# Two graph-attention layers on one core: whole-pair hops, second buffers for layer 2, and orders dealt anew

## The chip, the core and the metric

The kernel runs on one core of one Trainium2 chip. The metric is the device time of one execution in microseconds (us). TensorE is called PE, VectorE DVE, ScalarE ACT, GpSimd POOL and SyncE SP, as the profile does; PEld is TensorE's loading of weights.

## What is computed

There are 64 graphs of 128 nodes with 256 features, 8 heads of 32, all float32. Layer 0 (the diff's "layer 1") is masked attention with an output projection, a residual and a layer norm; layer 1 ("layer 2") computes probabilities in the same way and then spreads the values four times over the graph:

```python
# layer 0
q, k, v = x @ Wq + bq, x @ Wk + bk, x @ Wv + bv        # per head
attn = softmax(where(adj == 0, -inf, q k^T / sqrt(32)))
x = layernorm(x + (attn v) @ Wo + bo) * gamma + beta
# layer 1, on that x
q, k, v = x @ Wq.T + bq, x @ Wk.T + bk, x @ Wv.T + bv
pros = softmax(where(adj == 0, -16384, q k^T))
z = v
for _ in range(4):                                      # NUM_HOP
    z = 0.9 * pros z + 0.1 * v
out = layernorm(x + z) * gamma + beta
```

## The kernel before

Graphs are taken in 32 pairs, two graphs (b = 0, 1) at a time, so that 256 columns go through a projection. Each engine has a list of its own steps and no scheduler stands behind them: a function `step(t)` (lines 459, 636, 892 and 1031 for PE, ACT, DVE and POOL, and one for SP's loads and stores) names the operations in their order, each for the pair t, t - 1, ... t - 6, and `run` calls it for t = 0 to about 38. Operations whose pair isn't real fall away. So the beginning and the end of the program are the same list with holes in it. Semaphores, one `Count` for each kind of result, carry the order between engines.

For a pair and a layer l the chain is this. `queries`, `keys` and `values` on PE project x (six matmuls a call, since x and W are each split into a rounded high part and a low rest, and three of the four products are made; L326 and L335). `save_q`, `save_k` and `save_v` take the results out of PSUM. `scores` (L375) makes 16 products of 32 rows in the four banks of `psS`; `mask_scores` on DVE (L744, four calls of four heads) adds the mask and finds the maxima; `exp_two` on ACT (L603, eight calls of two heads) makes exponentials and sums; `reciprocals` on DVE (L753) and `probabilities` on POOL (L959) make the probabilities; `turn_probs` on PE (L385) transposes them, four heads a call, and `save_pT` (ACT L612, DVE L760) copies them to `pT`. In layer 0 `attend` (L393) multiplies with v, `save_oh` and `save_ol` split the result, `output` (L335) projects it, `save_y`, `statistics`, `aggregate`, `add_eps` (DVE), `inverse_root` (POOL L972) and `normalise` (DVE L835) make x1, `turn_x1` (L419) transposes it, and `save_x1h`, `save_x1l` split it for layer 1.

In layer 1 a hop is `hop` on PE (L393: for each head, 32 columns of z times pT, 32-wide weights), `save_hop` on ACT (L629, out of PSUM with the factor 0.9), `turn_hop` on PE (L437: two transposes back) and `add_hop` on DVE (L864: adds the restart term `z0s` or, in the fourth, the residual `zf`). All of these are called for one graph of the pair at a time, with 256 of a bank's 512 columns: `hop(j, b, p)`. `restart_term`, `last_term`, `scale_residual`, `shift_residual`, `scale_out`, `shift_out` and `add_bias` are POOL's. The last two pairs are finished by DVE alone (`finish`, L844 and L848).

Four PSUM banks, `F[0]` to `F[3]`, serve everything but scores. A table (lines 159 to 167) deals them out, and before each block PE waits in `free(...)` for the one evacuation that made the bank free. `folds` (L447, L455) multiplies biases into weights once. The seven raw weights lie in one tile `w_raw`, and layer 1's `pT`, `v` and `z0s` have one buffer each: `save_pT(1, ...)` of a pair waits until the last hop of the pair before is done, `save_v(1, p)` until its first hop and restart term are, and `restart_term(p)` for the third hop's sums of pair p - 1.

The order of a round on PE before (pair offsets left out) is: turn_probs(0,0,1); values(0); attend; hop 2; scores(0); turn_hop 2; output; hop 3; four turn_probs(1); values(1,0); hop 0; keys(0,0), values(1,1); turn_x1; keys(0,1); queries(0); turn_hop 3 and 0, one graph each; queries(1); keys(1,0); turn_hop 3 and 0 of the other graph; keys(1,1); turn_probs(0,1,1); hop 1; scores(1); turn_hop 1; turn_probs(0,1,0) and (0,0,0).

Of the kernel before, what the change touches and what calls it, by code (L numbers as in the profile page):

```python
# [13 lines left out]
HD = D // H  # L14
# [65 lines left out]
def two_layers(nc, x, x_t, adj, w, rows, cols, ident_d, out):  # L80
    ctx = ExitStack()
    with ctx:
# [15 lines left out]
        def over_jb(name):  # L98
            return [[count(f"{name}{j}_{b}") for b in range(2)] for j in range(NUM_HOP)]
# [5 lines left out]
        w_raw = sb("w_raw", [128, NW, C, D])  # L105
# [19 lines left out]

        xh = [sb(f"xh{l}", [128, C, T], F32R) for l in range(2)]
# [3 lines left out]
        v = [sb(f"v{l}", [128, 2, D]) for l in range(2)]  # L130
# [6 lines left out]
        pT = [sb(f"pT{l}", [128, 2, H, N]) for l in range(2)]  # L137
# [12 lines left out]
        z0s = sb("z0s", [128, 2, D])  # L150
        zf = [sb(f"zf{i}", [128, 2, D]) for i in range(4)]
        hT = [sb(f"hT{i}", [128, 2, C, N]) for i in range(2)]
# [6 lines left out]
        ps_q = [F[3], F[2]]  # L159
        ps_k = [F[1], F[0]]  # L160
        ps_v = [F[1], F[0]]
        ps_T = [[[F[0], F[2]], [F[3], F[2]]],
                [[F[0], F[3]], [F[2], F[1]]]]
        ps_av, ps_wo, ps_x1 = F[3], F[2], F[2]
        ps_h = [[F[3], F[2]], [F[1], F[3]], [F[2], F[0]], [F[1], F[3]]]
        ps_u = [[F[1], F[0]], [F[1], F[2]], [F[0], F[1]], [F[1], F[3]]]
        ps_fold_bo, ps_fold = F[3], F[1]
# [6 lines left out]
        avr = [count(f"av{b}_ready") for b in range(2)]  # L174
        wor = count("wo_ready", 2)
        x1r = count("x1T_ready")
        hr = over_jb("hopT_ready")
        zr = over_jb("hop_ready")
# [5 lines left out]
        hT_s = over_jb("hopT_saved")  # L184
# [16 lines left out]
        z_s = over_jb("hop_saved")  # L201
# [34 lines left out]

        def run(step, begin, end):
            for t in range(begin, end):
                step(Pair(t))
# [8 lines left out]
        def _(sp):  # L248
# [18 lines left out]
            def load_w(i):  # L267
                sp.dma_start(w_raw[:, i, :, :], w[i].rearrange("(c p) o -> p c o", p=128)).then_inc(w_in[i], 16)
# [12 lines left out]
            load_w(0)  # L281
            load_w(1)
            sp.dma_start(col[:, :, :], cols).then_inc(col_in, 16)
            load_adj(P0)
            load_w(2)
# [10 lines left out]
            def step(t):  # L296
                load_xt(t + 2)
                store(t - 5)
                load_x(t + 1)
                load_adj(t + 2)  # L300

            run(step, 0, PAIRS + 5)
# [4 lines left out]
        def _(pe):  # L307
# [9 lines left out]
            def weight(p, i):  # L317
                if p.is_(0):
                    pe.wait_ge(wh_s, i + 1)
                    pe.wait_ge(wl_s, i + 1)  # L320
# [68 lines left out]
            def spread(l, b, dst, o, src, done):  # L389
                for c in range(C):  # L390
                    for g in range(G):
                        h = G * c + g
                        last = nc.tensor.matmul(dst[32 * g:32 * g + 32, o + c * N:o + (c + 1) * N],  # L393
                                                src[:, b, h * HD:(h + 1) * HD], pT[l][:, b, h, :],
                                                start=True, stop=True)
                last.then_inc(done.sem, 1)

            def attend(b, p):
                if p.real:
                    pe.wait_ge(v_s[0].sem, v_s[0].at(p))  # L400
                    pe.wait_ge(pT_s[0][b][0].sem, pT_s[0][b][0].at(p))
                    pe.wait_ge(pT_s[0][b][1].sem, pT_s[0][b][1].at(p))
                    spread(0, b, ps_av, b * D, v[0], avr[b])
# [19 lines left out]
            def hop(j, b, p):  # L423
                if p.real:
                    if j:
                        pe.wait_ge(z_s[j - 1][b].sem, z_s[j - 1][b].at(p))
                    else:
                        pe.wait_ge(v_s[1].sem, v_s[1].at(p))
                        pe.wait_ge(pT_s[1][b][0].sem, pT_s[1][b][0].at(p))
                        pe.wait_ge(pT_s[1][b][1].sem, pT_s[1][b][1].at(p))  # L430
                    spread(1, b, ps_h[j][b], 0, z[p.parity] if j else v[1], hr[j][b])

            def turn_hop(j, b, p):
                if p.real:
                    pe.wait_ge(hT_s[j][b].sem, hT_s[j][b].at(p))
                    for c in range(C):
                        last = nc.tensor.transpose(ps_u[j][b][:, c * 128:(c + 1) * 128], hT[p.parity][:, b, c, :],  # L437
                                                   ident[:, :])
                    last.then_inc(zr[j][b].sem, 1)

            def folds():

                pe.wait_ge(sc_s, 1)
                for n, i in ((0, 3), (1, 6)):
                    pe.wait_ge(w_in[i], 16)
                    for kc in range(C):
                        last = nc.tensor.matmul((ps_fold_bo, ps_fold)[n][:, :D], spread_col[:, n, kc, :],  # L447
                                                w_raw[:, i, kc, :], start=(kc == 0), stop=(kc == C - 1))
                    last.then_inc(fold_r, 1)
                for n, i in ((0, 4), (1, 5)):  # L450
                    pe.wait_ge(w_in[i], 16)
                    for c in range(C):
                        o = D + n * C + c
                        for kc in range(C):
                            last = nc.tensor.matmul(ps_fold[:, o:o + 1], w_raw[:, i, kc, c * 128:(c + 1) * 128],  # L455
                                                    col[:, BE0c, kc:kc + 1], start=(kc == 0), stop=(kc == C - 1))
                last.then_inc(fold_r, 1)

            def step(t):
                free((z_s[1][1], t - 5), (pT_s[0][1][1], t - 2))  # L460
                turn_probs(0, 0, 1, t - 2)
                free((z_s[1][0], t - 5), (hT_s[1][0], t - 5), (z_s[0][0], t - 5), (z_s[3][0], t - 6), (k_s[0], t - 1))
                values(0, 0, t - 1)
                values(0, 1, t - 1)
                free((pT_s[0][1][0], t - 2))
                attend(0, t - 2)
                attend(1, t - 2)
                free((pT_s[0][0][0], t - 2), (k_s[1], t - 3), (z_s[0][1], t - 5))
                hop(2, 1, t - 5)
                free((pT_s[0][0][1], t - 2), (z_s[1][1], t - 5))  # L470
# [606 lines left out]
```

## Time and profile before

| what | value |
|---|---|
| three runs | 815.98, 816.67 and 817.33 us, median 816.67 |
| the profiled execution | 817.31 us, its span 815.4 us |
| mean granted TensorE clock over the span | 0.983 of full |
| busy: PE, ACT, DVE, POOL | 94%, 84%, 81%, 68% of the span |
| chain that ended last | PE 91%, DVE 4%, issue 3%, ACT 1%, DMA 1% |
| DMA | 34.19 MB, mean 42 GB/s |

The span is the time from the first to the last instruction of the program in the profile. Matmuls are pipelined, so that two may overlap in the rows: their starts are to be compared, not their ends. Idle time is counted in front of the instruction that ended it, with the engine and line that it waited for.

### The profile page before, as it was taken

To read this page: it belongs to the slowest core of one execution; us is meant where nothing else is said; L and a number is where in the kernel's file an instruction comes from. 1 tells how busy PE (TensorE), PEld (TensorE's weight loads), DVE (VectorE), ACT (ScalarE), POOL (GpSimd) and SP (SyncE) were. 2 spreads that over 40 slices of the span, in tenths; PEclk is the share of its full clock that TensorE was granted. 3 is DMA by queue.
4 is the path that set the end of the run, shared out by engine and by line. 5 is a ranking of instruction groups with operands and counts; after the bars stand their busy time and mean duration, and the time that the engine had idled before them with its cause. 6 is when DMAs were issued, how large, how long until landed. Compare 5 with 4: busy or idle time off the path is not lost.

```text
span 815.4 us, 33295 instructions
## 1 busy us (share of the span) xinstructions
PE 769.7 (94%) x11544; PEld 710.5 (87%) x11544; DVE 658.4 (81%) x3253; ACT 687.0 (84%) x2698; POOL 554.7 (68%) x417
## 2 busy tenths in 40 slices
PE   5678999999999999999999999999999999998873
PEld 5677999999999999999999999999999999997762
DVE  2578778888888888888888888888888888888745
ACT  3558999889998998899899989898998898989661
POOL 0245666777877777777777777787777777777662
PEclk9789999999999999999999999999999999999998
DMA  6101100111011111110111111011111110110001
GB/s 217 34 27 41 28 23 2 48 48 46 11 41 48 47 48 47 49 36 15 47 49 47 49 48 47 17 33 48 47 48 48 47 48 16 35 35 28 16 22 46
DMA packets 33252, 34.19 MB, mean 42 GB/s; under 512 B 2368, under 2 KB 28864, under 8 KB 33088
## 3 DMA queue, kind: packets, MB, share of 16 engines
q1 hardware_dynamic: 33088, 32.06, 12.9%
q8 instruction: 96, 1.57, 0.9%
q14 instruction: 68, 0.56, 0.2%
HBM read 23.67 MB, written 8.39 MB: 39 GB/s over the span
## 4 chain that ended last, share of the span: by engine, by line
PE 91%; DVE 4%; issue 3%; ACT 1%; DMA 1%; SPq 0%; POOLq 0%; DVEq 0%; ACTq 0%
PE psF L326 23%; PE psF L393 19%; PE psF L335 17%; PE psF L385 14%; PE psS L375 8%; PE psF L437 8%; PE psF L419 2%; DMA w_raw<-in_w 1%; DVE z L864 0%; ACT ex L603 0%; DVE sm L744 0%; ACT hT L629 0%; DVE w_lo L689 0%; ACT oh L621 0%; DVE y L791 0%
## 5 line engine op out<-in xcount | busy, mean ns | idle before, releaser
L603 ACT ACTIVATE ex<-sm,nmax 128x128 f32<-128x128 f32 x1024 | 396.9, 395 | 13.4 <-DVE nmax L744 13.4
L959 POOL TENSOR_TENSOR pr<-ex,rec 128x1024 f32<-128x1024 f32 x128 | 244.5, 1911 | 109.2 <-DVE rec L753 105.5
L744 DVE CUSTOM_DVE_ANT_0 sm<-psS,mask 128x128 f32<-128x128 f32 x1024 | 226.1, 284 | 4.6 <-PE psS L375 4.6
L603 ACT ACTIVATION_READ_ACCUMULATOR ex<-sm,nmax 128x1 f32 x1024 | 198.1, 193 | 0.0
L612 ACT ACTIVATE pT<-psF 128x512 f32<-128x512 f32 x192 | 104.7, 598 | 47.4 <-PE psF L385 47.4
L385 PE MATMUL psF<-ident,pr 128*128 128x128 f32 x1024 | 132.2, 278 | 5.0 <-issue 3.8
L326 PE MATMUL psF<-xh,w_hi 128*128 128x256 f32 x512 | 114.9, 306 | 15.5 <-DVE w_lo L685 7.6
L385 PEld LDWEIGHTS psF<-ident,pr 128*128 128x128 f32 x1024 | 115.4, 143 | 12.2 <-issue 11.4
L629 ACT ACTIVATE hT<-psF 128x256 f32<-128x256 f32 x256 | 95.1, 387 | 22.1 <-PE psF L393 16.7
L972 POOL TENSOR_TENSOR rstd<-ve,mhalf 128x2 f32<-128x2 f32 x64 | 55.5, 867 | 83.9 <-DVE ve L823 83.9
L864 DVE TENSOR_TENSOR z<-psF,z0s 128x256 f32<-128x256 f32 x192 | 76.5, 412 | 41.2 <-PE psF L437 41.0
L393 PE MATMUL psF<-pT,z 128*32 128x128 f32 x3072 | 103.4, 275 | 3.8 <-DVE z L864 3.2
L326 PE MATMUL psF<-xh,w_lo 128*128 128x256 f32 x512 | 104.3, 286 | 0.0
L326 PE MATMUL psF<-xl,w_hi 128*128 128x256 f32 x512 | 104.3, 286 | 0.0
L326 PEld LDWEIGHTS psF<-xh,w_hi 128*128 128x128 f32 x512 | 79.9, 194 | 21.8 <-issue 20.2
L393 PEld LDWEIGHTS psF<-pT,z 128*32 128x32 f32 x3072 | 80.6, 110 | 14.6 <-issue 9.3
L437 PE MATMUL psF<-ident,hT 128*128 128x128 f32 x512 | 82.0, 280 | 7.1 <-ACT hT L629 2.1
L744 DVE DVE_READ_ACCUMULATOR2_ANT nmax<- 128x1 f32 x1024 | 85.1, 83 | 0.0
L326 PEld LDWEIGHTS psF<-xl,w_hi 128*128 128x128 f32 x512 | 80.8, 194 | 0.0
L326 PEld LDWEIGHTS psF<-xh,w_lo 128*128 128x128 f32 x512 | 80.5, 194 | 0.0
L375 PE MATMUL psS<-kT,qT 32*128 32x128 f32 x2048 | 75.1, 283 | 0.9 <-DVE kT L733 0.9
L375 PEld LDWEIGHTS psS<-kT,qT 32*128 32x128 f32 x2048 | 63.0, 186 | 13.6 <-issue 13.5
(68 smaller groups left out, 1422.2 us busy)
## 6 DMA issues: line engine op xcount, KB each, us to landing
xt_in<-in_x_t SPq DMA_DIRECT2D x32, 256.0 KB, 3.3
x_in<-in_x SPq DMA_DIRECT2D x32, 256.0 KB, 3.7
out<-o_t SPq DMA_DIRECT2D x30, 256.0 KB, 3.0
adj_in<-in_adj SPq DMA_DIRECT2D x32, 128.0 KB, 3.0
w_raw<-in_w SPq DMA_DIRECT2D x7, 256.0 KB, 4.8
row<-in_rows SPq DMA_DIRECT2D x1, 768.0 KB, 6.4
out<-o_t SPq DMA_DIRECT2D x4, 128.0 KB, 1.7
ident<-in_ident SPq DMA_DIRECT2D x1, 64.0 KB, 3.8
```

What stands on the lines that cost most here:

```text
L326: last = nc.tensor.matmul(dst[:, c * T:(c + 1) * T], w_p[e][:, i, kc, c * 128:(c + 1) * 128], x_p[a][:, kc, :], start=(n == 0 and kc == 0) ...
L335: last = nc.tensor.matmul(dst[:, b * D:(b + 1) * D], x_p[a](kc), w_p[e][:, i, kc, :], start=(n == 0 and kc == 0), stop=(n == 2 and kc == C ...
L375: last = nc.tensor.matmul(psS[:, o:o + N], qT[l][r, c, b * N:(b + 1) * N], kT[l][r, c, b * N:(b + 1) * N], start=True, stop=True)
L385: last = nc.tensor.transpose(ps_T[l][b][c][:, g * N:(g + 1) * N], pr[l][:, b, G * c + g, :], ident[:, :])
L393: last = nc.tensor.matmul(dst[32 * g:32 * g + 32, o + c * N:o + (c + 1) * N], src[:, b, h * HD:(h + 1) * HD], pT[l][:, b, h, :], start=Tru ...
L437: last = nc.tensor.transpose(ps_u[j][b][:, c * 128:(c + 1) * 128], hT[p.parity][:, b, c, :], ident[:, :])
L603: e = nc.scalar.activation(ex[l][:, b, h, :], sm[l][:, b, h, :], ACT.Exp, scale=-1.0, bias=nmax[l][:, b, h:h + 1], accum_out=tot[l][:, b, ...
L612: nc.scalar.activation(pT[l][:, b, G * c:G * c + G, :], ps_T[l][b][c][:, :].rearrange("p (g n) -> p g n", g=G), ACT.Copy).then_inc(pT_s[l] ...
L629: nc.scalar.activation(hT[p.parity][:, b, :, :], ps_h[j][b][:, :D].rearrange("p (c n) -> p c n", c=C), ACT.Copy, scale=1.0 - ALPHA).then_i ...
L744: last = nc.vector.tensor_tensor_reduce(sm[l][:, b, h, :], psS[:, o:o + N], mask[p.parity][:, b, :], -1.0, BIG, ALU.add, ALU.min, nmax[l][ ...
L864: nc.vector.tensor_tensor(dst[:, b, :], ps_u[j][b][:, :D], add[:, b, :], ALU.add).then_inc(z_s[j][b].sem, 1)
L959: nc.gpsimd.tensor_tensor(pr[l][:, b, :, :], ex[l][:, b, :, :], rec[l][:, b, :].unsqueeze(2).broadcast_to([128, H, N]), ALU.mult).then_inc ...
```

## The change

- `w_raw` shrinks to weights 4 to 6. Weights 0 to 3 are loaded into what is later the second buffer of `pT` (`raw(i)`). Layer 1 gets two each of `pT`, `v` and `z0s`; the second `v` and `z0s` are `w_raw[1]` and `w_raw[0]`, once the weights have been read. The waits of `save_pT(1)`, `save_v(1)` and `restart_term` now look back two pairs.
- `hop`, `turn_hop`, `save_hop` and `add_hop` take both graphs of the pair in one call with a whole bank: 32 matmul records, four transposes, one operation on 512 columns. `attend` does so too. Semaphores per graph go.
- `save_hop(0)`, and layer 0's `save_k`, go from ACT to DVE; all eight `save_pT` and `save_x1h` go to ACT. `make_mask` is told which maxima read the mask last.
- Banks are dealt anew. Each compute engine's list is now a written-out `begin()`, a `step(t)` for t = 7 to 31 and a written-out `end()`; hops lie up to seven pairs back and stores nine. SP keeps its step with `store(t - 9)`.
- In the rounds, hop 1 of one pair and hop 3 of the pair before stand on either side of `attend`, and hop 0 and hop 2 of two pairs are neighbours.

```diff
-        w_raw = sb("w_raw", [128, NW, C, D])
+        w_raw = [sb(f"w_raw{i}", [128, C, D]) for i in range(4, NW)]
...
+        def raw(i):
+            if i < 4:
+                return pT1[1][:, i // 2, 4 * (i % 2):4 * (i % 2) + 4, :].rearrange("p (c o) n -> p c (o n)", c=C)
+            return w_raw[i - 4][:, :, :]
...
+        v1 = [sb("v1", [128, 2, D]), w_raw[1]]
+        z0s = [sb("z0s", [128, 2, D]), w_raw[0]]
+        pT1 = [sb(f"pT1_{i}", [128, 2, H, N]) for i in range(2)]
...
+        ps_q = [F[0], F[3]]
+        ps_k = [F[2], F[1]]
+        ps_v = [F[0], F[2]]
+        ps_T = [[[F[3], F[3]], [F[2], F[1]]],
+                [[F[0], F[3]], [F[1], F[3]]]]
+        ps_av, ps_wo, ps_x1 = F[1], F[1], F[1]
+        ps_h = [F[0], F[3], F[2], F[2]]
+        ps_u = [F[2], F[0], F[0], F[3]]
...
+            def hop(j, p):
+                if p.real:
+                    if j:
+                        pe.wait_ge(z_s[j - 1].sem, z_s[j - 1].at(p))
+                    else:
+                        pe.wait_ge(v_s[1].sem, v_s[1].at(p))
+                        for saved in pT_s[1][0] + pT_s[1][1]:
+                            pe.wait_ge(saved.sem, saved.at(p))
+                    spread(pT1[p.parity], ps_h[j], z[p.parity] if j else v1[p.parity], hr[j])
...
+            def step(t):
+                free((z_s[2], t - 7))
+                values(0, 0, t - 2)
+                free((mx[0][1][0], t - 3))
+                scores(1, t - 4)
+                free((pT_s[0][0][1], t - 3))
+                turn_probs(0, 0, 0, t - 3)
...
+                turn_probs(0, 1, 1, t - 3)
+                values(0, 1, t - 2)
+                free((pT_s[0][0][0], t - 3))
+                hop(1, t - 6)
+                free((pT_s[0][1][1], t - 3))
+                attend(t - 3)
+                free((pT_s[0][1][0], t - 3))
+                hop(3, t - 7)
+                free((mx[1][1][0], t - 4))
+                scores(0, t - 2)
+                free((hT_s[1], t - 6))
+                turn_probs(1, 0, 1, t - 5)
+                free((v_s[0], t - 2))
+                turn_hop(1, t - 6)
+                free((ol_s, t - 3))
+                output(0, t - 3)
+                output(1, t - 3)
+                free((z_s[1], t - 6))
+                queries(0, 0, t - 1)
...
+                values(1, 1, t - 4)
+                free((y_s, t - 3))
+                turn_probs(1, 1, 0, t - 5)
...
+                free((v_s[1], t - 4))
+                keys(0, 0, t - 1)
+                keys(0, 1, t - 1)
+                free((pT_s[1][1][1], t - 5))
+                turn_hop(3, t - 7)
+                free((pT_s[1][1][0], t - 5))
+                turn_x1(t - 3)
+                free((pT_s[1][0][0], t - 5))
+                hop(0, t - 5)
+                free((k_s[0], t - 1))
+                hop(2, t - 6)
+                free((z_s[3], t - 7))
+                queries(1, 0, t - 3)
+                queries(1, 1, t - 3)
+                free((x1l_s, t - 3))
+                keys(1, 0, t - 3)
+                free((hT_s[0], t - 5))
+                turn_hop(2, t - 6)
+                keys(1, 1, t - 3)
+                free((hT_s[2], t - 6))
+                turn_hop(0, t - 5)
+                free((q_s[1], t - 3))
                 turn_probs(0, 0, 1, t - 2)
...
+            def end():
...
+                hop(3, Pair(31))
+                free((z_s[3], Pair(30)))
+                turn_hop(3, Pair(31))
+
+            begin()
+            run(step, 7, PAIRS)
+            end()
...
             def step(t):
...
+                save_q(0, t)
                 add_eps(0, t - 2)
+                normalise(1, 0, t - 8)
+                mask_scores(0, 1, 1, t - 1)
                 normalise(0, 1, t - 2)
                 normalise(0, 0, t - 2)
+                reciprocals(1, 0, t - 3)
+                normalise(1, 1, t - 8)
+                save_k(0, t)
+                aggregate(1, t - 7)
+                add_hop(3, t - 6)
                 save_x1l(t - 2)
+                save_hop(0, t - 4)
                 reciprocals(0, 0, t - 1)
+                add_eps(1, t - 7)
```

PE's `begin()` starts with queries, keys and values of pair 0 and its scores, then the folds; DVE's starts with make_mask, save_q, save_k and maxima of pair 0 ahead of `save_fold`. In DVE's `end()`, `finish` of pair 30 stands ahead of `add_hop(3, Pair(31))`.

## Rows read from the trace of the kernel before

**Rows 1.** The page, part 1: busy time, share of the span, instructions.

```profile
PE 769.7 (94%) x11544; PEld 710.5 (87%) x11544; DVE 658.4 (81%) x3253; ACT 687.0 (84%) x2698; POOL 554.7 (68%) x417
```

**Rows 2.** Busy time by stage: stage, its length, engines, TensorE's granted clock, DMA share, GB/s.

```profile
core 0: us, PE busy (x) PEld busy (x) DVE busy (x) ACT busy (x) POOL busy (x), PEclk, DMA share, GB/s
7.60:47.10 39.50, 27.40 (x226) 25.47 (x226) 19.76 (x80) 18.00 (x63) 6.56 (x4) 0.83 0.28 93
...
111.10:742.40 631.30, 631.30 (x9717) 587.63 (x9716) 542.42 (x2722) 572.45 (x2266) 468.76 (x349) 1.00 0.13 40
742.40:778.00 35.60, 28.75 (x463) 25.05 (x464) 27.26 (x130) 25.86 (x109) 24.72 (x20) 1.00 0.03 10
```

**Rows 3.** Timeline of TensorE (start us, us taken): the transposes of x1.

```profile
47.15 1.09 PE L419 MATMUL psF<-ident,xn 128*128 128x128 f32 x4
...
67.86 0.60 PE L419 MATMUL psF<-ident,xn 128*128 128x128 f32 x4
...
88.13 0.60 PE L419 MATMUL psF<-ident,xn 128*128 128x128 f32 x4
...
111.13 0.60 PE L419 MATMUL psF<-ident,xn 128*128 128x128 f32 x4
...
719.70 0.60 PE L419 MATMUL psF<-ident,xn 128*128 128x128 f32 x4
```

**Rows 4.** Timeline of TensorE, one round: equal neighbours are merged.

```profile
448.22 1.47 PE L385 MATMUL psF<-ident,pr 128*128 128x128 f32 x12
...
450.49 0.40 PE L335 MATMUL psF<-w_lo,xh 128*128 128x256 f32 x2
450.73 0.40 PE L335 MATMUL psF<-w_hi,xl 128*128 128x256 f32 x2
451.06 1.08 PE L393 MATMUL psF<-pT,v 128*32 128x128 f32 x32
451.96 1.06 PE L393 MATMUL psF<-pT,z 128*32 128x128 f32 x32
452.94 1.17 PE L375 MATMUL psS<-kT,qT 32*128 32x128 f32 x32
...
456.06 1.08 PE L393 MATMUL psF<-pT,z 128*32 128x128 f32 x32
457.07 1.97 PE L385 MATMUL psF<-ident,pr 128*128 128x128 f32 x16
...
462.23 0.60 PE L419 MATMUL psF<-ident,xn 128*128 128x128 f32 x4
462.58 0.48 PE L326 MATMUL psF<-xh,w_hi 128*128 128x256 f32 x2
```

**Rows 5.** Timelines of ScalarE and VectorE in the same round: what reads PSUM.

```profile
448.85 1.58 ACT L612 ACTIVATE pT<-psF 128x512 f32<-128x512 f32 x3 [0.95 <-PE psF L385]
...
448.87 0.28 DVE L744 CUSTOM_DVE_ANT_0 sm<-psS,mask 128x128 f32<-128x128 f32 x1
...
452.24 0.20 DVE L753 RECIPROCAL rec<-tot 128x8 f32<-128x8 f32 x1
...
462.87 0.69 DVE L768 CAST xh<-psF 128x512 fp32r<-128x512 f32 x1 [0.47 <-PE psF L419]
```

**Rows 6.** Timelines of GpSimd and VectorE: probabilities, and a weight split beside one.

```profile
28.90 1.89 POOL L959 TENSOR_TENSOR pr<-ex,rec 128x1024 f32<-128x1024 f32 x1 [1.84 <-DVE rec L753]
...
29.14 2.20 DVE L685 TENSOR_TENSOR w_lo<-w_raw,w_hi 128x512 fp32r<-128x512 f32 x1 [0.32 <-ACT w_hi L557]
...
452.52 1.96 POOL L959 TENSOR_TENSOR pr<-ex,rec 128x1024 f32<-128x1024 f32 x1 [1.27 <-DVE rec L753]
```

**Rows 7.** Timelines of several engines: the beginning and the end.

```profile
4.84 0.69 DVE L685 TENSOR_TENSOR w_lo<-w_raw,w_hi 128x512 fp32r<-128x512 f32 x1 [0.18 <-ACT w_hi L557]
...
28.10 0.39 ACT L603 ACTIVATE ex<-sm,nmax 128x128 f32<-128x128 f32 x1
...
806.30 0.63 PE L437 MATMUL psF<-ident,hT 128*128 128x128 f32 x4 [0.91 <-ACT hT L629]
...
807.42 0.47 DVE L844 SCALAR_TENSOR_TENSOR o_t<-y,mv,row 128x256 f32<-128x256 f32 x1
```

More of the change, by code:

```diff
@@ L96, in over_bc, with over_j @@
             return [[[count(f"{name}{l}_{b}{c}") for c in range(C)] for b in range(2)] for l in range(2)]
-        def over_jb(name):
-            return [[count(f"{name}{j}_{b}") for b in range(2)] for j in range(NUM_HOP)]
+        def over_j(name):
+            return [count(f"{name}{j}") for j in range(NUM_HOP)]
         P0, P1 = Pair(0), Pair(1)
@@ L148, in two_layers @@
         xn = [sb(f"xn{i}", [128, 2, D]) for i in range(2)]
-        z0s = sb("z0s", [128, 2, D])
         zf = [sb(f"zf{i}", [128, 2, D]) for i in range(4)]
-        hT = [sb(f"hT{i}", [128, 2, C, N]) for i in range(2)]
+        hT = [sb(f"hT{i}", [128, 2 * C, N]) for i in range(2)]
         z = [sb(f"z{i}", [128, 2, D]) for i in range(2)]
@@ L235, in two_layers, with turn @@
         block = ctx.enter_context(nc.Block())
+        W_ORDER = (0, 1, 2, 3, 4, 5, 6)
+        def turn(i):
+            return W_ORDER.index(i) + 1
         def run(step, begin, end):
@@ L297, in step @@
                 load_xt(t + 2)
-                store(t - 5)
+                store(t - 9)
                 load_x(t + 1)
                 load_adj(t + 2)
-            run(step, 0, PAIRS + 5)
+            run(step, 0, PAIRS + 9)
             for p in (Q, R):
@@ L679, in _ @@
+            begin()
+            run(step, 7, PAIRS)
+            end()
         @block.vector
@@ L689, in split_w @@
                         last = nc.vector.scalar_tensor_tensor(
-                            out=w_lo[:, i, kc, :], in0=w_raw[:, i, kc, :], scalar=col[:, GA0c, kc:kc + 1],
+                            out=w_lo[:, i, kc, :], in0=raw(i)[:, kc, :], scalar=col[:, GA0c, kc:kc + 1],
                             in1=w_hi[:, i, kc, :].bitcast(FP32), op0=ALU.mult, op1=ALU.subtract)
@@ L796, in statistics @@
                     if l:
[L797 to L798 removed]
+                        dve.wait_ge(z_s[NUM_HOP - 1].sem, z_s[NUM_HOP - 1].at(p))
                     else:
@@ new lines, in step @@
+            def step(t):
+                mask_scores(0, 1, 0, t - 2)
+                save_q(1, t - 3)
+                add_hop(2, t - 6)
+                reciprocals(0, 1, t - 2)
+                save_k(1, t - 3)
+                add_hop(0, t - 5)
+                statistics(1, t - 7)
+                mask_scores(1, 0, 0, t - 3)
+                reciprocals(1, 1, t - 4)
+                mask_scores(1, 1, 1, t - 3)
+                mask_scores(1, 0, 1, t - 3)
+                mask_scores(1, 1, 0, t - 3)
+                make_mask(t - 1)
+                split_lo(t)
+                save_ol(t - 2)
+                mask_scores(0, 0, 1, t - 1)
+                add_hop(1, t - 5)
+                mask_scores(0, 0, 0, t - 1)
+                save_y(t - 2)
+                statistics(0, t - 2)
@@ L949, in _ @@
+            begin()
+            run(step, 7, PAIRS)
+            end()
         @block.gpsimd
@@ L1049 @@
+            begin()
+            run(step, 7, PAIRS)
+            end()
 def kernel(**inputs):
```

1473 lines of the change are left out of this document (1171 added, 302 removed).

## The prediction

> **What bounds the kernel now.** I read the page's busy times first, then the stages, then TensorE's timeline. TensorE (PE) is busy 94% of the span, ScalarE (ACT) 84%, VectorE (DVE) 81% [rows 1]. By stage it is plainer: from 111 to 742 us PE is busy all of the time at full clock, while ACT is busy 572 and DVE 542 of 631 us; before 47 us and after 742 us it is not, and its clock is below full before 47 us [rows 2]. The transposes of x1, one block a pair, stand at 111.13 and 719.70 with 26 pairs between: 23.41 us a round, PE's own sum [rows 3]. The kernel is three parts: a filling to about 111 us, rounds of 23.41, a draining after 742. Thirty-two rounds and the folds (3.4 us) are 752.5 us of PE work; the other 63 of the 815.4 us are standing, slow clock and the ends.
>
> A round has 14 projections of six matmuls (P), 52 transposes, five blocks of 32-wide matmuls over both batches (attention and four hops, H) and two score blocks (S). From start to start: two matmuls of P take 0.24 us, so P 0.71; twelve transposes last 1.47 and four 0.60, so 0.109 each, four 0.44 (T). An H block that stands alone takes 1.01 (456.06 to 457.07), two in a row 1.88 (451.06 to 452.94): so H is 0.87 and **each run of H blocks costs 0.14 beside it**. S takes 1.10 (its 1.17 less the 0.07 by which an H's 1.08 is over its spacing). Going from P into such a block costs 0.09 (450.73 to 451.06 is 0.33 in place of 0.24); sixteen transposes behind an H last 1.97 where twelve last 1.47, 0.50 for four in place of 0.44, so the return to T costs 0.06 [rows 4]. Summed with four runs this gives 23.3, the round but for rounding.
>
> **Part 1, the round's order on PE.** No matmul is added or dropped. Before, the tiled blocks stand in four places: (A, hop 2, S), (hop 3), (hop 0), (hop 1, S). After, in three: (S), (hop 1, A, hop 3, S), (hop 0, hop 2). Two H runs fewer, 0.28; one entry from P fewer, 0.09; one return to T fewer, 0.06. That is 0.42 a round: 22.99. The 25 rounds of the new step give 10.5; counting the places in the written-out beginning and end in the same way, PE's whole work falls by 12.6. S alone behind P has no row in the stretch of rounds; its price lies between nothing saved (a further 0.1 lost) and 0.1 gained, 2.5 us in all either way, and I take the S of rows 4.
>
> **Part 2, whether the others keep up.** ACT loses eight hop evictions of 256 and layer 0's two of keys and gets three of 512, two of pT and x1's high part: a 512 eviction steps 0.49 (three in 1.58) [rows 5], so 2.9 us go in; a 256 one steps between half of that and all of it, so 2.5 to 4.9 go out. I take the middle, about 0.7 less. DVE gets save_k(0) and save_hop(0), gives up two pT and x1h, and sums 512 four times in place of 256 eight times: at least one 0.6 less. GpSimd (POOL) does the same. So per round neither is asked for more than before, which was 572 and 542 of 631 us, 21.2 and 20.1 of 23.41 [rows 2], and both fit in 22.99. SP's queue has the same DMAs; stores come up to four rounds later and each output tile is still taken only after its store.
>
> What matters is each hand-over. A PSUM reader starts 0.29 us after the block's end (462.58 to 462.87), sixteen masked maxima take 3.37 (448.87 to 452.24), a DVE 512 takes 0.60 to 0.69 [rows 4, 5]. With the prices above I laid the new round on a ruler (values(0,0) at 0): S1 0.9 to 2.0, hop 1 4.1, A 5.0, hop 3 5.9, S0 6.95 to 8.0, turn of hop 1 8.45, queries 10.3, values(1,1) ends 13.1, transposes 13.1 to 14.5, keys 14.5, turn of hop 3 15.9, x1 16.3 to 16.8, hop 0 16.9, hop 2 17.7, layer 1's queries 18.84, turn of hop 0 22.1. The tight ones: **S0** needs layer 1's maxima, 2.1 + 3.4 + a reciprocal 0.1 = 5.7 of 6.95; **queries** need hop 1's sum, 8.9 + 0.3 + 0.7 = 9.9, and their weights load from 10.1: 0.2 spare; **keys** need v1 saved, 13.1 + 0.3 + 0.6 = 14.0 of 14.3; **layer 1's queries** need x1's low part: ACT 17.04 to 17.55, DVE (behind keys 16.8, aggregate 17.0, hop 3's sum 17.6) 17.6 to 18.3, with loading from 18.6: 0.3 spare. Attention behind four pT evictions has 0.8, hop 2's bank 0.6. So no wait is left on PE, but four margins are 0.2 to 0.3. The second buffers of pT, v and z0s are costed at nothing: no row of a round shows PE waiting, and what they bring is the right to hold hops of pair p while pair p + 1 is saved; without them the order could not be.
>
> **Part 3, the filling.** The queries come first and need only weight 0, whose low part is ready at 5.5 (4.84 + 0.69) [rows 7]; PE started at 7.6 [rows 2]: 2 gained. Then DVE does all of pair 0's maxima before the folds, so exps end at about 21 in place of 28.5 (28.10 + 0.39) [rows 7]. Walking on with the same prices: probabilities by POOL to 23.8, raw weights rounded to 24.0, four pT to 26.5, attention 26.6, output from 29.3, y behind the weight splits 32.3, statistics and root 34.3, x1 of pair 0 at **35.3** in place of 47.15. Pair 1 at 53.1 in place of 67.86 and pair 2 at 72.2 in place of 88.13 [rows 3]: between them PE stands at score blocks for maxima and at x1 for the root, 0.5 to 1.2 a time. From there 26.2 us of PE work reach the first round; with 1 for clock and small waits it begins at 99.5.
>
> **Part 4, the draining.** The written-out end holds 84.3 us of PE work to its last turn. Waits, by the same prices: scores of pair 31 for maxima 0.5, x1 of pair 30 for its root 1.0, keys of pair 31 for x1 0.7, and the last hops 5.6: a whole-pair hop is H, 0.3 + 0.5 on ACT, T, 0.3 + 0.7 on DVE, 3.2 us, where pair 30's hop beside it fills 1.3, and at the very end nothing does. So 92.1. Then sum, statistics, root, two finishing operations a batch and the store. From the last turn to the end it was 9.1 (806.30 to 815.4) [rows 7]; pair 30's finishing, four DVE operations of about 0.47 that stood in this path for 1.8, now comes ahead of the last sum: 7.6, and 0.3 for that sum's delay. Total 100.0.
>
> **Sum.** 99.5 + 25 x 22.99 + 100.0 = 774.3. Waits that a hand walk misses can only add; I add 2.2: a span of 776.5. The profiled run took 817.31 for its span of 815.4, 1.9 more: 778.4, and the median of the runs lies 0.6 below it: **778 us** against 816.7. Of the 39 gained, 12.6 are PE's own prices and 26 the two ends.
>
> **The rivals.** (a) *The margins fail a little*: a hand-over of 0.2 spare comes late by 0.2 to 0.6 each round, 5 to 15 us: 783 to 793. For it: four such places, and DVE and ACT both serve each x1. Against: 2 to 4 us of slack in both engines' sums. (b) *The ends give half*: the filling's clock stays low longer (0.83 there now [rows 2]) or a fixed order stands for one late engine; 13 us back: 791.
>
> (c) *The lock, on the slower side.* DVE operations with SBUF operands alone and POOL's work exclude each other here: w_lo that takes 0.69 took 2.20 when it began inside a probabilities operation of 28.90 to 30.79 [rows 6, 7]. In the new round the second output normalise(1,1) stands right behind reciprocals(1,0), which releases POOL's 1.9 us probabilities(1,0), and ahead of keys, hop 3's sum and x1's low part. If POOL wins that race, DVE is 1.9 late there, the 0.3 spare is used up and layer 1's queries wait 1.6: 25 x 1.6 = 40 us, 818. It decides from 1.55 a round on (38.7 / 25). Against it: DVE issues at once, while POOL starts 0.08 behind the reciprocal's end (452.24 + 0.20 to 452.52) [rows 5, 6], so DVE should get in first.
>
> The Trainium skill, SBUF — State Buffer, section "SBUF: two separate sides", says that the port pair of these two engines is an exclusive lock and that whichever starts first has it for its whole instruction. By that rule the trace agrees (2.20 for 0.69), and rival (c) would give about 818 wherever POOL is first.
>
> **How the numbers follow.** Forecast (span within 6 us of the sum) 0.62, its own range 771 to 786; (a) 0.17; (b) 0.13; (c) 0.04; better than 770, 0.04. The range 770 to 795 takes in the forecast, (a) and most of (b) and leaves out (c). About 0.2% is what a measurement can tell here, and only (c) comes near it or past: faster 0.95, within 0.01, slower 0.04.
>
> **What would show it.** x1's blocks at 35, 53 and 72 us and then 22.99 apart; PE busy 100% from about 100 to 690 at clock 1.0; last turn some 7.6 ahead of the end. Part 1 is wrong if an unwaited round isn't 22.99; part 2 if PE's gaps recur each round; (c) if w-type DVE operations of 2 us recur each round.

## The result and the profile after

The changed kernel took **783.1 us** (median of four runs, 782.6 to 786.1) against 816.8 of the kernel before: a ratio of 0.960, 95% interval 0.9585 to 0.9612. The forecast was 778.0 with a range of 770 to 795. The profiled run was the longest of the four, 786.14 us with a span of 784.0, and a second profile of the same kernel has a span of 781.1. Of the 2.9 us between the two, 2.3 arise in the first 38 us, so both are shown.

The page, part 1, of the kernel after:

```profile
span 784.0 us, 32528 instructions
...
PE 754.1 (96%) x11544; PEld 710.6 (91%) x11544; DVE 637.1 (81%) x3093; ACT 665.7 (85%) x2570; POOL 547.8 (70%) x417
```

Against [rows 1], PE has the same 11544 matmuls and is busy 15.6 us less in a span that is 31.4 us shorter; ACT's and DVE's busy times are 21 us less each. Next, busy time by stage, first of the profiled run, with the columns of [rows 2]: filling to pair 0's x1, filling to the first generic round, 25 rounds, two stretches of the draining.

```profile
5.60:37.90 32.30, 29.20 (x250) 26.88 (x250) 23.80 (x102) 21.49 (x82) 7.44 (x5) 0.89 0.43 140
37.90:103.10 65.20, 61.99 (x804) 57.08 (x805) 51.23 (x261) 55.49 (x223) 38.88 (x28) 1.00 0.12 34
103.10:677.20 574.10, 574.10 (x9001) 547.00 (x8999) 482.41 (x2393) 514.45 (x2003) 424.83 (x319) 1.00 0.14 40
677.20:736.00 58.80, 57.45 (x951) 53.17 (x950) 49.20 (x246) 52.52 (x200) 45.53 (x37) 1.00 0.08 25
736.00:775.00 39.00, 30.79 (x541) 26.19 (x542) 23.40 (x81) 19.83 (x65) 30.17 (x25) 0.96 0.09 29
```

And the same stages of the second profile:

```profile
5.60:35.70 30.10, 25.80 (x251) 23.44 (x252) 23.60 (x103) 21.16 (x82) 7.43 (x5) 1.00 0.46 145
35.70:100.70 65.00, 62.05 (x804) 57.11 (x805) 50.27 (x260) 55.57 (x223) 38.94 (x28) 1.00 0.12 35
100.70:674.70 574.00, 574.00 (x8999) 546.90 (x8998) 482.32 (x2392) 514.42 (x2002) 425.36 (x319) 1.00 0.14 40
```

In the rounds PE is busy for 574 of 574 us at full clock: a round is 22.96 us. ACT works 20.6 and DVE 19.3 us in each, so both stay below it. Between the two profiles the first stage differs most: at clock 0.89 it took 2.2 us longer than at 1.00, for the same 250 matmuls.

The timeline of PE, the transposes of x1 (start us, us taken), of the kernel after:

```profile
37.93 0.63 PE L436 MATMUL psF<-ident,xn 128*128 128x128 f32 x4
56.46 0.69 PE L436 MATMUL psF<-ident,xn 128*128 128x128 f32 x4 [0.15 <-issue]
75.88 0.66 PE L436 MATMUL psF<-ident,xn 128*128 128x128 f32 x4
...
693.54 0.60 PE L436 MATMUL psF<-ident,xn 128*128 128x128 f32 x4
```

With [rows 3], this splits the gain of the profiled run: 88.13 − 75.88 = 12.3 us are won by pair 2's x1; the 27 intervals from there to pair 29's take 617.7 in place of 631.6, so 13.9 (27 × 0.45 = 12.2 are the shorter round, the rest is the way into it); and from there to the end it is 90.5 in place of 95.7, so 5.2. Together 31.4.

| us | before | forecast | after, profiled | after, second profile |
|---|---|---|---|---|
| x1 of pair 0 / 1 / 2 | 47.2 / 67.9 / 88.1 | 35.3 / 53.1 / 72.2 | 37.9 / 56.5 / 75.9 | 35.7 / 54.1 / 73.4 |
| a round | 23.41 | 22.99 | 22.96 | 22.96 |
| start of the draining to the last turn | another list | 92.1 | 97.7 | 97.3 |
| last turn to the end | 9.1 | 7.6 | 9.1 | 9.0 |
| span | 815.4 | 776.5 | 784.0 | 781.1 |

### The profile page after: what moved, and what is told of

The parts are those of the page before. It is cut to its first block, busy times and chain, and to the rows that moved or that the text cites. A ratio compares the mean times of both kernels' runs of the same rounds, so it can differ in the third digit from the quotient of the medians.

```text
span 784.0 us, 32528 instructions
## 1 busy us (share of the span) xinstructions
PE 754.1 (96%) x11544; PEld 710.6 (91%) x11544; DVE 637.1 (81%) x3093; ACT 665.7 (85%) x2570; POOL 547.8 (70%) x417
## 4 chain that ended last, share of the span: by engine, by line
PE 89%; DVE 3%; ACT 2%; issue 2%; DMA 1%; SPq 1%; POOL 1%; POOLq 0%; DVEq 0%; ACTq 0%
PE psF L342 23%; PE psF L411 18%; PE psF L351 16%; PE psF L401 15%; PE psS L391 9%; PE psF L456 7%; PE psF L436 2%; ACT ex L1011 2%; DMA w_raw<-in_w 1%; DVE sm L1400 1%; DMA out<-o_t 1%; SPq L284 0%; DVE o_t L1491 0%; DVE bst L1450 0%; POOL o_t L1927 0%
## 5 line engine op out<-in xcount | busy, mean ns | idle before, releaser
L1011 ACT ACTIVATION_READ_ACCUMULATOR ex<-sm,nmax 128x1 f32 x1024 | 200.7, 196 | 0.0
L1022 ACT ACTIVATE pT<-psF 128x512 f32<-128x512 f32 x256 | 138.8, 596 | 34.5 <-PE psF L401 34.4
L401 PE MATMUL psF<-ident,pr 128*128 128x128 f32 x1024 | 137.8, 276 | 0.8 <-ACT pT L1022 0.5
L401 PEld LDWEIGHTS psF<-ident,pr 128*128 128x128 f32 x1024 | 112.7, 141 | 9.3 <-ACT pT L1022 0.9
L342 PE MATMUL psF<-xh,w_hi 128*128 128x256 f32 x512 | 112.6, 302 | 7.7 <-DVE w_lo L1339 5.7
L411 PEld LDWEIGHTS psF<-pT,z 128*32 128x32 f32 x3072 | 84.2, 111 | 8.1 <-issue 3.5
L1880 POOL TENSOR_TENSOR xb<-x_in,bo_row 128x512 f32<-128x512 f32 x32 | 41.7, 1302 | 70.2 <-DVE y L1439 52.9
L456 PE MATMUL psF<-ident,hT 128*128 128x128 f32 x512 | 76.4, 273 | 5.7 <-DVE hT L1416 3.9
L1872 POOL TENSOR_TENSOR rstd<-ve,mhalf 128x2 f32<-128x2 f32 x64 | 47.2, 737 | 43.5 <-DVE ve L1470 43.3
L1045 ACT ACTIVATE hT<-psF 128x512 f32<-128x512 f32 x96 | 57.0, 596 | 18.1 <-PE psF L411 18.0
```

Source lines behind the costliest of these rows:

```text
L342: last = nc.tensor.matmul(dst[:, c * T:(c + 1) * T], w_p[e][:, i, kc, c * 128:(c + 1) * 128], x_p[a][:, kc, :], start=(n == 0 and kc == 0) ...
L401: last = nc.tensor.transpose(ps_T[l][b][c][:, g * N:(g + 1) * N], pr[l][:, b, G * c + g, :], ident[:, :])
L411: last = nc.tensor.matmul(dst[32 * g:32 * g + 32, o:o + N], src[:, b, h * HD:(h + 1) * HD], p_T[:, b, h, :], start=True, stop=True)
L456: last = nc.tensor.transpose(ps_u[j][:, o:o + 128], hT[p.parity][:, b * C + c, :], ident[:, :])
L1011: e = nc.scalar.activation(ex[l][:, b, h, :], sm[l][:, b, h, :], ACT.Exp, scale=-1.0, bias=nmax[l][:, b, h:h + 1], accum_out=tot[l][:, b, ...
L1022: nc.scalar.activation(pT[l][p.parity][:, b, G * c:G * c + G, :], ps_T[l][b][c][:, :].rearrange("p (g n) -> p g n", g=G), ACT.Copy).then_i ...
```

## The experiments

The theory after the result had three parts: the round is PE's own sum, by prices per run of tiled blocks; the filling's order brings about 13 us; the draining is longer than forecast because VectorE stands for stores and for GpSimd. The rivals: the round's worth lies in its hand-overs, the written-out ends bring nothing, or VectorE's waits there are covered.

**One merge undone.** Hop 3 leaves its run with hop 1 and attention and stands alone between the two blocks of the output projection; ScalarE saves it later. Nothing is added or dropped.

```diff
 PE, step(t)
-                free((pT_s[0][1][0], t - 3))
-                hop(3, t - 7)
...
                 output(0, t - 3)
+                free((pT_s[0][1][0], t - 3))
+                hop(3, t - 7)
                 output(1, t - 3)
```

> In the rounds hop 3 stands alone between the two output projections, and its eviction on ACT four operations later. No work is added; there is one more run of 32-wide blocks a round. Theory: an entry 0.09, a run 0.14 and a return to projections 0.11 more, 0.34 a round, so 23.30 a round and 8.5 us in 25 rounds: 791 to 792 us. Rival (the places of the blocks cost nothing by themselves): 783.

Measured: 794.4 us, ratio to before 0.973 (0.9716 to 0.9745), so 11.3 over the kernel after; rounds of 23.33, 0.37 more. The timeline of PE in one round of it:

```profile
460.50 0.48 PE L351 MATMUL psF<-w_hi,oh 128*128 128x256 f32 x2
...
461.05 0.40 PE L351 MATMUL psF<-w_hi,ol 128*128 128x256 f32 x2
461.38 1.08 PE L411 MATMUL psF<-pT,z 128*32 128x128 f32 x32
462.39 0.50 PE L351 MATMUL psF<-w_hi,oh 128*128 128x256 f32 x2
...
463.20 0.41 PE L342 MATMUL psF<-xh,w_hi 128*128 128x256 f32 x2
```

From 461.05 to 461.38 is 0.33 where two matmuls of a projection take 0.24: the entry costs 0.09 again. The block lasts 1.01 in place of 0.87 in a run, and the projection behind it (462.39 to 463.20, 0.81) 0.10 more than its 0.71. That is 0.33 of the 0.37. Over 25 rounds it gives 9.2 us; 1.6 more arose in the first two rounds (24.19 and 24.28 us), where PE waits for the low part of attention's result. The timelines of POOL, DVE and PE in the first of them:

```profile
106.41 1.96 POOL L1859 TENSOR_TENSOR pr<-ex,rec 128x1024 f32<-128x1024 f32 x1 [0.26 <-DVE rec L1409]
106.53 2.38 DVE L1357 TENSOR_TENSOR xl<-xt_in,xh 128x512 fp32r<-128x512 f32 x1
109.66 0.48 PE L351 MATMUL psF<-w_hi,oh 128*128 128x256 f32 x2 [0.81 <-DVE ol L1423]
```

DVE's split of x, 0.68 alone, lies beside POOL's probabilities there and takes 2.38, with `save_ol` queued behind it. The kernel after has the same slow split in these two rounds (2.39 and 1.76), but its PE comes to the output projection later and doesn't wait. In the other rounds PE waits for nothing: the same matmuls in another order cost more. The price of a run of tiled blocks stands.

**The beginning and the end made generic.** The first seven steps, the last steps, or both run the round's own list with the missing pairs left out. To let any order be safe, these kernels also have PE wait on every PSUM bank's last reader.

```diff
-            begin()
-            run(step, 7, PAIRS)
-            end()
+            run(step, 0, PAIRS + 8)
```

> The changed kernel's round, called from t = 0 to the last pair as the kernel before does it, in place of the written-out beginning and end (the folds and the weights' rounding are hung into its rounds 1 and 2). Theory: the rounds stay 22.96 us apart, and the ends cost at least what they cost before, since the same PE work (32 x 22.96 + 3.4 = 738 us) is left and the waits of both ends, 63 us before, come back, with three rounds more in flight: 800 to 815 us. Rival (the gain is the round's order and not the lists of the ends): within 5 us of 783.

> Only the beginning is the round called from t = 0; the written-out end stays. Theory: the first of the rounds begins some 14 us later (the first x1 near 47 to 50 us in place of 38), 795 to 800 us. Rival: the beginning is bound by the loads and by the first pair's own chain, and the time is within 4 us of 783.

> Only the end is the round called on to the last pair; the written-out beginning stays. Theory: the last pairs stand in a list made for full rounds and the end grows by 5 to 20 us, 788 to 803 us, more than the 5.6 us by which the waits of the end shrank, since hops now lie seven rounds back. Rival: the written-out end brings nothing, 783.

Measured: both 801.0 us (0.9797 to 0.9826 of before), beginning alone 800.5 (0.9791 to 0.9824), end alone 786.8 (0.9622 to 0.9651). All three carried a confound, the longer waits, so these were run alone, beside the kernel after once more:

```diff
+            def take(bank, reader, p):
+                before = last_use.get(id(bank))
+                if before is not None and before != (id(reader), p.number):
+                    for sem_, value in last_use[(id(bank), "wait")]:
+                        pe.wait_ge(sem_, value)
...
 scores(l, p)
+                    take(psS, mx_all[l], p)
```

> The changed kernel with nothing moved: only TensorE's waits on PSUM banks are the longer, generic ones that the kernels with plain ends used (two readers for the score bank, one wait more for each bank taken). Theory (the waits themselves cost PE's queue time): rounds of 23.1, the first round not later than 1 us, 786 to 788 us; then the plain end costs nothing by itself. Rival (it was the plain ends that lengthened the round, by what they leave behind): rounds of 22.96 and 783.

> The changed kernel itself, unchanged, as the measure for the two others of this call. Rounds of 22.96, the median within 1 us of 783.1. Open is the first stage: its 784.0 us profile had TensorE at half clock for 6.8 us from 17.4 and x1 of pair 0 at 37.9. If that stretch is no part of the kernel, another profile may show x1 of pair 0 at 35.3 to 36 and a span of 781.

Measured: with the waits alone 786.4 us (0.9619 to 0.9648), the kernel after 783.95 (0.9588 to 0.9633). So the generic end costs 786.8 − 786.4 = 0.4 us, nothing that can be told, where 5 to 20 had been expected, and the generic beginning 800.5 − 786.4 = 14.1. The written-out draining brings nothing beside the round's own list; the written-out filling is worth more than the 11 us of all the rounds' saving. The 14.1 are there by pair 3's x1 (108.1 for 94.1 with the waits alone; pair 0's came at 43.8 for 35.8, not at the 47 to 50 expected). Not all of it need be order: the kernels with a generic beginning also have the folds and the rounding of the later weights in rounds 1 and 2, and TensorE's granted clock was 0.87 up to 43.8 us and 0.96 from there to 127, against 1.00 in the same stages with the waits alone. These shares weren't separated.

The waits cost 2.5 to 3.3 us, but not in the way that was expected. With the waits alone the rounds are 22.96, but for eight of 23.05 to 23.99, all of them after 430 us, which hold 3.3 us more (the other three kernels with these waits have such rounds too). So the theory's even 23.1 is wrong though its total is right. The timeline of PE in the worst of them, in a score block:

```profile
452.25 0.48 PE L403 MATMUL psS<-kT,qT 32*128 32x128 f32 x3
453.28 1.16 PE L403 MATMUL psS<-kT,qT 32*128 32x128 f32 x29 [0.55 <-issue]
```

PE stands after a few matmuls of the block, 0.82 us from one to the next, where the profile shows no semaphore that it waits for. The program is longer by 126 instructions (32654 for 32528), and the kernel with the generic end, whose rounds are the same code, stands in the same block for the same 0.82 us. What comes late there the profile does not show; it stays open.

**One lock put in its place.** Rival (c) of the prediction did not occur. Here GpSimd is let in first: reciprocals(1, 0) stands ahead of the masks, so GpSimd's probabilities begin before the normalisations.

```diff
 DVE, step(t)
+                reciprocals(1, 0, t - 3)
                 mask_scores(0, 1, 1, t - 1)
                 normalise(0, 1, t - 2)
                 normalise(0, 0, t - 2)
-                reciprocals(1, 0, t - 3)
```

> In DVE's rounds reciprocals(1,0) stands four operations earlier, ahead of the maxima and of the two normalise(0) that x1 waits for; so POOL's probabilities(1,0) of 1.9 us begin before them. The work is the same. Theory of the lock: the two normalise(0), SBUF alone, are held until POOL's operation ends, at about 16.4 of the round in place of 14.7, x1 comes 0.9 to 1.3 late each round, and 25 rounds give 20 to 33 us: 803 to 816 us, with normalise operations of 1 us or more in the trace. Rival (no exclusion, only chance in the one slow operation before): 783, normalise still 0.41.

Measured: 801.3 us (0.9796 to 0.9825), 18.2 over the kernel after, and rounds of 23.59 to 23.65. The timelines of DVE and POOL in one of them:

```profile
445.73 2.31 DVE L1482 TENSOR_SCALAR xn<-y,mv,rstd 128x256 f32<-128x256 f32 x2
445.95 1.95 POOL L1859 TENSOR_TENSOR pr<-ex,rec 128x1024 f32<-128x1024 f32 x1 [0.49 <-issue]
```

and in a round of the kernel after:

```profile
462.08 0.73 DVE L1482 TENSOR_SCALAR xn<-y,mv,rstd 128x256 f32<-128x256 f32 x2
462.73 0.19 DVE L1409 RECIPROCAL rec<-tot 128x8 f32<-128x8 f32 x1
462.84 0.36 DVE L1482 TENSOR_SCALAR o_t<-y,mv,rstd 128x256 f32<-128x256 f32 x1
463.00 1.96 POOL L1859 TENSOR_TENSOR pr<-ex,rec 128x1024 f32<-128x1024 f32 x1 [1.12 <-DVE rec L1409]
```

Two normalisations that take 0.73 took 2.31 with a POOL operation begun inside them, ahead of the second: 1.6 us of DVE a round. But only 0.67 of it reached the round, less than the 0.9 to 1.3 expected: PE waits 0.5 at x1 and the rest lies in slack. In the kernel after, DVE is in first, 0.16 us ahead of POOL, in all 23 rounds in which they meet (in the first two no output is due yet). The Trainium skill, SBUF — State Buffer, section "SBUF: two separate sides", states an exclusive lock held for a whole instruction; the trace agrees here with its 2.31 and 0.73.

**One buffer of z0s.** For pairs 8 to 26 the second buffer isn't used; GpSimd's two operations on it change places in the round so that the order stays possible.

```diff
+        def z_at(p):
+            return 0 if 8 <= p.number <= 26 else p.parity
...
-                        dst, add = z[p.parity], z0s[p.parity]
+                        dst, add = z[p.parity], z0s[z_at(p)]
```

> Pairs 8 to 26 share one buffer of z0s in place of two; restart_term and last_term stand later in POOL's round so that the order is still possible. Theory: the second buffer of z0s buys only freedom of order, the round stays at 22.96 or within 0.1 of it, and the time within 3 us of 783. Rival (the second buffer takes a wait out of each round): 0.3 us or more a round, 789 and up.

Measured: 785.0 us (0.9599 to 0.9631), 1.9 over the kernel after, 1.0 over its second measurement; rounds of 22.96 but for two of 23.7 where the buffer changes and PE waits 0.5 for attention's low part. In the rounds the second z0s buys nothing but a free choice of order. The same was not tried for pT and v: by the order of the lists, with one buffer the new order would wait for a block that stands behind the waiting one, and the kernel would stop.

**The draining.** In the kernel after, DVE's timeline around pair 31's hop 0 is

```profile
761.04 0.73 DVE L1482 TENSOR_SCALAR o_t<-y,mv,rstd 128x256 f32<-128x256 f32 x2 [4.40 <-DMA out<-o_t]
761.69 0.68 DVE L1512 TENSOR_TENSOR y<-psF,zf 128x512 f32<-128x512 f32 x1
762.29 0.68 DVE L1416 TENSOR_SCALAR hT<-psF 128x512 f32<-128x512 f32 x1
```

and PE's, which waits for that hT:

```profile
763.12 1.06 PE L456 MATMUL psF<-ident,hT 128*128 128x128 f32 x8 [2.29 <-DVE hT L1416]
```

DVE stood 4.4 us for the store of pair 26 before it could write pair 28's output, with the eviction of the hop queued behind. Why the store was late, POOL's timeline shows:

```profile
745.38 1.28 POOL L1921 TENSOR_TENSOR o_t<-o_t,row 128x512 f32<-128x512 f32 x1
...
757.50 1.28 POOL L1927 TENSOR_TENSOR o_t<-o_t,row 128x512 f32<-128x512 f32 x1
```

Pair 26's output was scaled by 746.7, but its shift stands in POOL's `end()` behind eight more operations, two of them probabilities, and began at 757.50; the store follows it. Moving that shift forward was not tried. So the two output normalisations of pair 28 were put behind that eviction, and in a second kernel GpSimd's shift of pair 29 was moved ahead of its root of pair 30 too, to free DVE's last finishing from the lock:

```diff
 DVE, end()
-                normalise(1, 0, Pair(28))
-                normalise(1, 1, Pair(28))
...
                 save_hop(0, Pair(31))
+                normalise(1, 0, Pair(28))
+                normalise(1, 1, Pair(28))
 POOL, end(), second kernel only
+                shift_out(Pair(29))
                 inverse_root(1, Pair(30))
...
-                shift_out(Pair(29))
```

> In DVE's written-out end, pair 28's two output normalises, which wait for the store of pair 26, stand behind the first hop's eviction of pair 31 in place of ahead of it. Theory: the eviction no longer stands behind a store, and PE's 2.3 us ahead of that turn shrink to 0.3: 2 us less, ratio to the changed kernel 0.9975, 781 us. Rival: the wait moves on to the later sums, and the end stays.

> As the one before it, and POOL shifts pair 29's output ahead of pair 30's root in place of behind it, so that it isn't beside pair 30's finishing on DVE. Theory: the finishing operation that took 1.47 us takes 0.47, the root comes 0.4 later, 0.5 us less than the one before it. Rival: the same time, and 1.47 stays.

Measured: 783.5 us (0.9576 to 0.9605) and 783.0 (0.9578 to 0.9606): nothing. In the first, PE and DVE read

```profile
759.65 1.06 PE L456 MATMUL psF<-ident,hT 128*128 128x128 f32 x8 [0.91 <-DVE hT L1416]
761.82 1.96 PE L411 MATMUL psF<-pT,z 128*32 128x128 f32 x64 [1.10 <-DVE z L1512]
...
769.94 1.21 PE L411 MATMUL psF<-pT,z 128*32 128x128 f32 x32 [2.20 <-DVE z L1512]
```

```profile
767.54 0.74 DVE L1482 TENSOR_SCALAR o_t<-y,mv,rstd 128x256 f32<-128x256 f32 x2 [1.61 <-DMA out<-o_t]
```

The wait of 2.29 shrank to 0.91. A fall of TensorE's clock is gone too: in the kernel after, in its second profile and in two of the other kernels it is at half for 3.4 us that begin at the wait's end or within 2 us of it; in these two kernels it stays at full until the last turn, which takes 1.09 for 0.63. That the wait brings the fall isn't shown: three other kernels have the wait and no fall. But one pair later a wait of 2.20 stands where there was one of 0.88, behind pair 29's output and the store of pair 27, and the two hops in between (761.82) start 0.6 later behind their turn, 2.17 for 1.52. By the last turn the first kernel is 0.3 us ahead of the second profile of the kernel after, counted from the draining's start (97.0 for 97.3). The second kernel did to the lock what it was meant to: pair 30's first finishing operation takes 0.48 in place of 1.47. But it begins later, behind the root that now comes behind the shift, and the last sum starts at 773.34 in place of 773.51, so next to nothing is left of it:

```profile
771.50 0.48 DVE L1491 SCALAR_TENSOR_TENSOR o_t<-y,mv,row 128x256 f32<-128x256 f32 x1 [1.83 <-POOL rstd L1872]
```

A third kernel takes the wait of 2.20 away: pair 31's sum of hop 2 goes ahead of pair 29's output and pair 30's statistics, and POOL's root of pair 30 ahead of its scaling of pair 29.

```diff
 DVE, end(), beside the edit of the first kernel
                 add_hop(3, Pair(30))
+                add_hop(2, Pair(31))
                 normalise(1, 1, Pair(29))
                 normalise(1, 0, Pair(29))
                 statistics(1, Pair(30))
                 aggregate(1, Pair(30))
-                add_hop(2, Pair(31))
 POOL, end()
-                scale_out(Pair(29))
                 inverse_root(1, Pair(30))
+                scale_out(Pair(29))
```

> As e_tail1, and in the draining pair 31's hop 2 is summed ahead of pair 29's output and pair 30's statistics; GpSimd takes pair 30's root ahead of pair 29's scaling. Theory (behind the last sums the end is VectorE's own list, not TensorE's): PE's 2.2 us wait ahead of hop 3 of pair 31 goes, its last turn comes 1.5 to 2 us earlier (770.0 to 770.4 in place of 771.93), but pair 30's finishing and the last sum behind it move by less: 0 to 0.7 us, the median within 0.7 of e_tail1's 783.5. Rival (TensorE's last turn sets the end): 1.5 to 2 us faster, 781.5 to 782.

Measured: 785.7 us, a ratio to before of 0.963 with a wide interval, 0.9596 to 0.9672, which overlaps the first kernel's: not faster, and 2.2 over it where at most 0.7 had been expected (its runs spread from 784.2 to 791.1). In the profiled runs PE's last turn came at 770.54 in place of 771.93, and the span was 782.2 in place of 780.9. DVE's timeline after it:

```profile
771.11 1.47 DVE L1491 SCALAR_TENSOR_TENSOR o_t<-y,mv,row 128x256 f32<-128x256 f32 x1 [0.80 <-POOL rstd L1872]
772.62 1.37 DVE L1495 SCALAR_TENSOR_TENSOR o_t<-o_t,rstd,row 128x256 f32<-128x256 f32 x1
...
774.82 0.68 DVE L1512 TENSOR_TENSOR y<-psF,zf 128x512 f32<-128x512 f32 x1
```

The 1.4 us that PE won bring nothing: the last sum (774.82) waits for pair 30's finishing in front of it, of which two operations now lie beside POOL's scaling and shift and take 1.47 and 1.37 in place of 0.48. Behind the last hop the end is DVE's and POOL's. None of the experiments beats the kernel after by what can be measured.

## Why the prediction was right, and where it was 5 us short

**Part 1, right.** 22.99 forecast, 22.96 measured, and one merge undone costs 0.37 a round by the same terms. (The three terms add up to 0.43, not 0.42; it changes nothing.) The price that no row had, S alone behind P, came out at the middle: 448.12 to 448.44 is 0.32, the entry of an H block, and then 1.10, S's own.

```profile
448.12 0.39 PE L351 MATMUL psF<-w_hi,xl 128*128 128x256 f32 x2
448.44 1.17 PE L391 MATMUL psS<-kT,qT 32*128 32x128 f32 x32
449.54 1.53 PE L401 MATMUL psF<-ident,pr 128*128 128x128 f32 x12
```

**Part 2, right.** No wait is left on PE in a round, and the margins of 0.2 to 0.3 held: rival (a) fell. The slack was larger than the forecast needed: 1.6 us of DVE lost a round brought 0.67. That the second buffers bring only the right to the order is shown for z0s.

**Part 3, right but for small waits.** In the second profile x1 of pair 0 came at 35.7 (35.3 forecast), of pair 2 at 73.4 (72.2), the first round at 100.7 (99.5). The stations of the walk fit too and not only its end: attention of pair 0 at 27.0 (26.6 forecast), the output projection at 29.7 (29.3). The profiled run has 2.3 us more by pair 0, while its clock stood at half from 17.4 to 24.2 us; with the same code it did not in the other. That is most of the 2.5 to 3.5 us between its 786.1 and the other runs.

**Part 4 is the step that failed.** "So 92.1" measured 97.7 in the profiled run. The 84.3 us of work in it hold; the waits did not. Taken from matmul to matmul, PE stands 11.7 us there where the prediction put 7.8 (0.5, 1.0, 0.7 and 5.6), and 1.8 more go to a lower clock, which it did not put down at all. Two pairs of equal lines of PE's timeline of the kernel after show the clock:

```profile
751.74 1.06 PE L456 MATMUL psF<-ident,hT 128*128 128x128 f32 x8 [0.94 <-DVE hT L1416]
753.24 1.96 PE L411 MATMUL psF<-pT,z 128*32 128x128 f32 x64 [0.44 <-DVE z L1512]
...
764.64 3.38 PE L411 MATMUL psF<-pT,z 128*32 128x128 f32 x64 [0.46 <-DVE z L1512]
767.96 1.48 PE L456 MATMUL psF<-ident,hT 128*128 128x128 f32 x8
```

Two hops that take 1.96 took 3.38, eight transposes 1.48 for 1.06: 1.8 in all. 97.7 less 11.7 and 1.8 leaves 84.2, the work as forecast. Some 8.2 of the 11.7 lie in the last hops, from 749.7 on, for which the prediction had 5.6. The largest single piece stems from one omission: the prediction put SP's stores at nothing, "each output tile still taken only after its store", and named no one who waits for that. In the rounds nobody does. In the draining POOL's list has the shift of an output far behind its scaling, and DVE stands 4.4 us in its own queue ahead of what PE needs; PE stands 2.3 for it. A turn behind a hop waits 0.94 anyway (751.74), so the store accounts for 1.4 of the 3.9 us that weren't foreseen; the rest is spread over small waits. (The lower clock begins 2 us behind, but isn't tied to the wait by the runs.) The experiments show that taking this wait away alone gives nothing, since the next pair's output does the same. And in the kernel with the generic end DVE waits for no store at all, yet it isn't faster: the wait for the store belongs to the written-out lists, and by itself it isn't what makes the draining long.

"7.6" from the last turn to the end measured 9.1. The sum itself is unclear there: 9.1 less 1.8 is 7.3, so the 7.6 seems to hold the 0.3 for the last sum's delay already, and the total of 100.0 counts it again. The four finishing operations of pair 30 took 2.9 us, not 1.8, one of them 1.47 beside a POOL operation, and they stood in front of the last sum, which began 1.7 us after the last turn. DVE's timeline of the kernel after:

```profile
773.79 1.47 DVE L1491 SCALAR_TENSOR_TENSOR o_t<-y,mv,row 128x256 f32<-128x256 f32 x1 [0.81 <-POOL rstd L1872]
775.30 0.48 DVE L1495 SCALAR_TENSOR_TENSOR o_t<-o_t,rstd,row 128x256 f32<-128x256 f32 x1
...
776.62 0.68 DVE L1512 TENSOR_TENSOR y<-psF,zf 128x512 f32<-128x512 f32 x1
```

So the lock, which the prediction weighed as a rival for the rounds, was left out where it did act, in the last microseconds. It isn't the whole miss: with the lock gone in the second kernel of the draining, the last sum still began 1.7 us behind the last turn, since all of pair 30's finishing stands in front of it. By the second profile the sum stands thus: filling 100.7 for 99.5, rounds 574.0 for 574.8, draining 106.4 for 100.0 with 2.2 for unseen waits beside it: 781.1 for 776.5. The reserve of 2.2 had no source, and it and the 0.8 of the rounds made the miss of the sum smaller than that of its worst part: that the span came out within 5 us is in part luck.

**The rivals.** (b), half of the ends given back, fell: the filling kept nearly all of its own, and the draining missed by 6.4 us, not 13. (c) is right as a mechanism, and its race was won in the rounds. Its price, 1.6 a round and 818, wasn't tested: the experiment holds other operations, where 1.6 us of DVE cost PE 0.67 and the whole run 18.

## What to carry to other kernels

When one engine is always busy and others have slack, price the transitions between its kinds of blocks from the trace (here 0.14 for a run of tiled blocks, 0.09 into it, 0.06 to 0.10 out of it) and merge runs: that alone foretold 0.45 us a round to within 0.03. Write out a beginning by hand, where the order decides how soon the bound engine has work, and don't expect as much of an end: two reorderings there moved a wait from pair to pair, a third took it from PE, and none shortened anything. In a hand walk of a draining, put down for each buffer who frees it and what stands behind the wait on the same engine.

## What the runs showed of the hardware that was not expected

- PE stood 0.3 to 0.8 us inside a score block, behind 96 short tiled matmuls, with no semaphore open, in three to five of the later rounds of each of the four kernels whose program was 126 instructions longer, in two of them at the same matmuls; the kernel after has not one such gap.
- The same kernel had TensorE at half clock for 6.8 us early in one run and not in another, worth 2.3 us at pair 0's x1. Late in the draining it fell to half for 3.4 us (1.8 us longer matmuls in the kernel after) at a wait of 2.2 to 2.3 us in four profiles of the changed kernels, while three others with the same wait and those without it show no fall. What decides it stays open.
- A DVE operation of 0.36 us that begins 0.16 us ahead of POOL's 1.96 us one costs nothing, and a pair of them into which the POOL operation falls took 2.31 in place of 0.73: which of two engines is first by a sixth of a microsecond decides 1.6 us. It needn't show at once: a split of x held to 2.39 us costs the kernel after nothing, and 0.8 us once one merge of PE's blocks is undone.
